# A state-space and attention stack in elements: first elements with their own banks, division of work and order

## The reference

```
xz = x @ in_proj; xb, z = split(xz)                    # 256 + 256 channels
xb = silu(causal_depthwise_conv(xb, 4 taps) + conv_b)  # called u in the kernel
proj = xb @ x_proj;  dt = softplus(proj[:8] @ dt_proj + dt_b);  b, c = proj[8:24], proj[24:40]
state = exp(dt * a) * state + dt * b * xb              # 256 channels x 16 states, along 512 tokens
y = (sum over states of state * c + D * xb) * silu(z);  return y @ out_proj
```

## Time and profile before

| | us |
|---|---|
| median of 3 runs | 2429.0 |
| lowest, highest | 2427.78, 2432.51 |
| profiled execution: its own time | 2435.31 |
| its span | 2433.5 |
| mean granted TensorE clock | 0.923 of full |
| busy: PE, DVE, ACT, POOL | 1903.3, 1883.9, 1767.4, 1715.1 |

### The profile page before, as it was taken

How to read it: one execution, slowest core, us unless ns; L and a number is a source line. 1 busy time by engine, 2 the same in 40 slices (tenths; PEclk the granted TensorE clock), 3 DMA queues, 4 the chain that set the end, 5 groups by cost and what they waited for, 6 DMA issues and landing times.

```text
span 2433.5 us, 43992 instructions
## 1 busy us (share of the span) xinstructions
PE 1903.3 (78%) x15823; PEld 1130.5 (46%) x15936; DVE 1883.9 (77%) x3461; ACT 1767.4 (73%) x3955; POOL 1715.1 (70%) x1572
## 2 busy tenths in 40 slices
PE   2246789796978879697878979698887979788866
PEld 0013455363635546363645536364544636364634
DVE  3557797979878797988879797987879798887442
ACT  2345778696978878696877869697887869686644
POOL 1969595977959596886959597795959688693110
PEclk7566999899999999998999989999999989999988
DMA  5444343535445343634535363544535263540100
GB/s 171 122 121 116 102 121 98 144 93 132 108 118 132 93 125 81 151 89 127 136 95 121 96 143 93 135 105 118 131 97 127 78 158 88 138 112 20 26 20 9
DMA packets 126345, 261.08 MB, mean 107 GB/s; under 512 B 26928, under 2 KB 59696, under 8 KB 125872
## 3 DMA queue, kind: packets, MB, share of 16 engines
q1 hardware_dynamic: 126128, 258.27, 40.9%
HBM read 185.42 MB, written 42.99 MB: 94 GB/s over the span
## 4 chain that ended last, share of the span: by engine, by line
PE 30%; POOL 24%; DVE 21%; ACT 13%; issue 8%; DMA 3%; SPq 1%; POOLq 0%; DVEq 0%; ACTq 0%
POOL dbu L662 9%; POOL gy L679 9%; DVE hs L634 4%; POOL kr L996 4%; PE b_bank L358 3%; PE f_bank L358 3%; DVE m L927 3%; ACT late L892 3%; DVE kr L941 2%; PE y_sum L585 2%; PE b_bank L719 2%; DMA spread<-steps 2%; DVE ss L914 2%; PE b_bank L745 2%; PE f_bank L1027 2%
## 5 line engine op out<-in xcount | busy, mean ns | idle before, releaser
L634 DVE TENSOR_TENSOR_SCAN hs<-da,dbu 128x512 f32<-128x512 f32 x512 | 623.2, 1217 | 101.4 <-POOL dbu L662 68.9
L662 POOL TENSOR_TENSOR dbu<-spread,bc 128x512 f32<-128x512 f32 x512 | 653.6, 1277 | 27.5 <-DMA spread<-steps 27.4
L679 POOL TENSOR_TENSOR gy<-hs,bc 128x512 f32<-128x512 f32 x512 | 652.7, 1275 | 22.4 <-DVE hs L634 10.6
L610 ACT ACTIVATE da<-spread,rest 128x512 f32<-128x512 f32 x512 | 364.3, 712 | 160.1 <-DVE hs L634 130.6
L996 POOL TENSOR_TENSOR kr<-kr,rn 128x512 f32<-128x512 f32 x256 | 264.5, 1045 | 23.3 <-ACT rn L850 13.2
L719 PE MATMUL b_bank<-rest,h_t 128*128 128x512 f32 x384 | 232.7, 716 | 60.3 <-DVE kr L941 56.3
L719 PE MATMUL f_bank<-rest,h_t 128*128 128x512 f32 x384 | 217.9, 666 | 25.9 <-DVE kr L941 17.9
L585 PE MATMUL y_sum<-gy,rest 128*32 128x512 f32 x1024 | 147.2, 650 | 101.0 <-POOL gy L679 101.0
L358 PE MATMUL b_bank<-first,kr 128*128 128x128 f32 x768 | 128.0, 292 | 109.1 <-DVE kr L941 90.5
L358 PE MATMUL f_bank<-first,kr 128*128 128x128 f32 x768 | 126.5, 291 | 72.8 <-DVE kr L941 65.4
L358 PEld LDWEIGHTS b_bank<-first,kr 128*128 128x128 f32 x768 | 89.3, 147 | 191.9 <-DVE kr L941 145.8
(11 more groups left out here) (172 smaller groups left out, 4884.6 us busy)
## 6 DMA issues: line engine op xcount, KB each, us to landing
spread<-steps SPq DMA_DIRECT2D x256, 512.0 KB, 5.2
vs<-v SPq DMA_DIRECT2D x96, 260.0 KB, 6.9
steps<-k_t SPq DMA_DIRECT2D x32, 512.0 KB, 3.3
bc<-bc_rows SPq DMA_DIRECT2D x32, 512.0 KB, 6.3
gate<-gates SPq DMA_DIRECT2D x32, 512.0 KB, 6.3
gates<-kr SPq DMA_DIRECT2D x16, 512.0 KB, 2.7
gates<-late SPq DMA_DIRECT2D x16, 512.0 KB, 3.4
vs<-v SPq DMA_DIRECT2D x32, 130.0 KB, 5.5
```

The source lines that it names most:

```text
L610: e.activation(da[:, :], spread[:, slot(b, s // 2), 0, :], ACT.Exp, scale=a_neg[:, s:s + 1]).then_inc(decayed.sem, 1)
L634: e.tensor_tensor_scan(hs[:, s % 2, :], da[:, :], dbu[:, s % 2, :], 0.0, ALU.mult, ALU.add).then_inc(scanned.sem, 1)
L662: e.tensor_tensor(dbu[:, s % 2, :], spread[:, slot(b, s // 2), 1, :], bc[:, s % 2, :], ALU.mult).then_inc(fed.sem, 1)
L679: e.tensor_tensor(gy[:, s % 8, :], hs[:, s % 2, :], bc[:, 2 + s % 2, :], ALU.mult).then_inc(read_out.sem, 1)
```

## The change

Five things change. Line numbers of the new code are given where they differ.

1. **Entry of element 0.** The four input products write four banks (`fa[0]`, `fa[1]`, `fa[2]`, `lb[0]`), the projection to b, c and dt a fifth (`lb[1]`), the two dt products `fa[0]` and `fa[1]` again. PE's waits on the convolution and on z fall away; the projection waits for u alone.
2. **Step inputs of element 0** (dt and du, four products) run on DVE at the end of its entry, not on GpSimd.
3. **Read-out by DVE.** In element 0 the scans with s % 3 > 0 (21 of 32), in element 1 those with s % 3 == 1 (11 of 32) have their product with c on DVE, one place behind the next scan. Scan s then waits on DVE's own read-out of s - 2, and two semaphores count the read-outs of elements 0 and 1.
4. **Decays.** In elements 0 and 1 odd scans take their decay from the bank `lb[0]`, even ones from `da`, so the decay s waits for scan s - 2 and no longer for s - 1. The back attention of element 0 waits for the last scan of element 1 before it uses `lb[0]`.
5. **Order in three parts.** Each engine has three words: the first covers the first five rounds, the second is repeated 11 times, the third holds the rest. The steps in each part add up to what the old word gave there, but for one or two steps at the seams; inside a round steps move.

```diff
+ROUNDS = 11
-def weave(word, late, **chains):
+def weave(first, usual, last, **chains):
+    for word in (first, *[usual] * ROUNDS, last):
...
+        def entry_bank(b, part):
+            if b:
+                return e_bank
+            return dict(turn=e_bank, i0=fa[0], i1=fa[1], i2=fa[2], i3=lb[0], x=lb[1], d0=fa[0], d1=fa[1])[part]
...
+                if b == 0 and h == NH2 - 1:
+                    for _ in step_inputs(E, e, 0):
+                        pass
...
-                E.wait_ge(*before)
-                e.matmul(e_bank[:, :], w_in[:, i * P:(i + 1) * P], xn_t, start=True, stop=True).then_inc(in_projected.sem, 1)
+                E.wait_ge(*(before if b else e_copied(0)))
+                e.matmul(entry_bank(b, f"i{i}")[:, :], w_in[:, i * P:(i + 1) * P], xn_t, start=True, stop=True).then_inc(in_projected.sem, 1)
                 yield
-            E.wait_ge(*z_made(b, 1))
+            E.wait_ge(*(z_made(b, 1) if b else u_made(0, 1)))
...
-                if h:
+                if h and b:
                     E.wait_ge(*dt_clipped(b, 0))
...
+        SHARED = 2
+        def by_dve(b, s):
+            return b < SHARED and (s % 3 > 0, s % 3 == 1,)[b]
...
+        def decay(b, s):
+            return lb[0] if b < 2 and s % 2 else da
...
-                if s:
+                if s and decay(b, s) is decay(b, s - 1):
                     E.wait_ge(*scanned(b, s - 1))
+                elif s > 1:
+                    E.wait_ge(*scanned(b, s - 2))
...
             for s in range(NSCAN):
+                if s > 1 and by_dve(b, s - 2):
+                    E.wait_ge(*reads(b, s - 2)[-1])
                 E.wait_ge(*decayed(b, s))
                 E.wait_ge(*fed(b, s))
...
+                if s and by_dve(b, s - 1):
+                    read_product(E, e, b, s - 1)
+                if s == NSCAN - 1 and by_dve(b, s):
+                    read_product(E, e, b, s)
                 yield
...
+                if bank is lb[0] and n == 2 and b == 0:
+                    E.wait_ge(*scanned(1, NSCAN - 1))
```

More of the change, by code:

```diff
@@ L94, in use_table @@
             self.e.preload_act_table_set(name)
-def weave(word, late, **chains):
-    late = {part[0]: int(part[1:]) for part in late.split()}
-    while chains:
+def weave(first, usual, last, **chains):
+    for word in (first, *[usual] * ROUNDS, last):
         for part in word.split():
             for _ in range(int(part[1:])):
-                if late[part[0]]:
-                    late[part[0]] -= 1
-                elif part[0] in chains and next(chains[part[0]], chains) is chains:
-                    del chains[part[0]]
+                next(chains[part[0]])
+    for chain in chains.values():
+        for _ in chain:
+            raise AssertionError("a step is left over")
 def build(nc, a, out):
@@ L412, in dve_enter @@
             for h in range(NH2):
+                bank = entry_bank(b, f"i{h}")
                 E.wait_ge(*pad_zeroed(b))
@@ L437, in pool_steps @@
                 yield
+        def pool_steps(E, e, b):
+            if b:
+                yield from step_inputs(E, e, b)
+            else:
+                for _ in range(2 * NH2):
+                    yield
         def pe_enter(E, e, b):
@@ L474, in act_enter @@
             for h in range(NH2):
+                bank = entry_bank(b, f"i{h}")
                 E.wait_ge(*in_projected(b, h))
-                if h:
+                if h and b:
                     E.wait_ge(*conv_step(b, 2))
-                e.activation(x_pad[:, h, NCONV - 1:], e_bank[:, :], ACT.Copy).then_inc(padded.sem, 1)
+                e.activation(x_pad[:, h, NCONV - 1:], bank[:, :], ACT.Copy).then_inc(padded.sem, 1)
                 E.wait_ge(*padded(b, h))
-                e.activation(e_bank[:, :], e_bank[:, :], ACT.Identity, bias=conv_b[:, h:h + 1],
+                e.activation(bank[:, :], bank[:, :], ACT.Identity, bias=conv_b[:, h:h + 1],
                              scale=conv_w[:, h, NCONV - 1:NCONV]).then_inc(tap_made.sem, 1)
@@ L497, in act_enter @@
                 E.wait_ge(*dt_projected(b, h))
-                e.activation(dt_abs[:, h, :], e_bank[:, :], ACT.Abs, bias=dt_b[:, h:h + 1]).then_inc(dt_size.sem, 1)
+                e.activation(dt_abs[:, h, :], entry_bank(b, f"d{h}")[:, :], ACT.Abs, bias=dt_b[:, h:h + 1]).then_inc(dt_size.sem, 1)
                 yield
@@ L509, in act_steps, with reads, read_product @@
             yield
+        SHARED = 2
+        def by_dve(b, s):
+            return b < SHARED and (s % 3 > 0, s % 3 == 1,)[b]
+        def reads(b, s):
+            if b >= SHARED:
+                return [read_out(b - SHARED, s)]
+            n = [0, 0]
+            for other in range(b + 1):
+                for step in range(s + 1 if other == b else NSCAN):
+                    n[by_dve(other, step)] += 1
+            return [sem(k - 1) for sem, k in ((pool_read, n[0]), (dve_read, n[1])) if k]
+        def read_product(E, e, b, s):
+            E.wait_ge(*c_loaded(b))
+            E.wait_ge(*scanned(b, s))
+            if s > 7:
+                E.wait_ge(*summed_up(b, 2 * (s // 8 - 1) + s % 2))
+            elif b > 0:
+                E.wait_ge(*x1_made(b - 1))
+            e.tensor_tensor(gy[:, s % 8, :], hs[:, s % 2, :], bc[:, 2 + s % 2, :], ALU.mult).then_inc(
+                (read_out if b >= SHARED else dve_read if by_dve(b, s) else pool_read).sem, 1)
         def group_rows(b, g):
@@ L543, in sp_state @@
             if b > 0:
-                E.wait_ge(*read_out(b - 1, NSCAN - 1))
+                for done in reads(b - 1, NSCAN - 1):
+                    E.wait_ge(*done)
             load_bc(1, c_loaded)
@@ L582, in pe_state @@
                     E.wait_ge(*skipped(b - 1, 1))
-                E.wait_ge(*read_out(b, 8 * (m // 2) + 6 + k))
+                for done in reads(b, 8 * (m // 2) + 6 + k):
+                    E.wait_ge(*done)
                 for j in range(4):
@@ L606, in act_state @@
                 E.wait_ge(*loaded(b, s // 2))
-                if s:
+                if s and decay(b, s) is decay(b, s - 1):
                     E.wait_ge(*scanned(b, s - 1))
+                elif s > 1:
+                    E.wait_ge(*scanned(b, s - 2))
                 E.use_table(EXP_LN)
-                e.activation(da[:, :], spread[:, slot(b, s // 2), 0, :], ACT.Exp,
+                e.activation(decay(b, s)[:, :], spread[:, slot(b, s // 2), 0, :], ACT.Exp,
                              scale=a_neg[:, s:s + 1]).then_inc(decayed.sem, 1)
@@ L672, in pool_state @@
                     yield
[L673 to L679 removed]
+                if not by_dve(b, s):
+                    read_product(E, e, b, s)
                 yield
```

31 lines of the change are left out of this document (10 added, 21 removed), and 81 rows, old and new, of the table ORDER.

## The result

| | before | after |
|---|---|---|
| median, us | 2430.8 (4 runs) | 2470.9 (4 runs) |
| lowest, highest | 2427.8, 2438.6 | 2464.1, 2474.5 |
| profiled execution, its span | 2435.3, 2433.5 | 2474.5, 2472.3 |
| ratio of after to before, 95% interval | | 1.0158 [1.0136, 1.0179] |

The change makes the kernel 1.6% slower. The forecast was 2389, so it missed by 82 us and named the wrong sign. The start gains 23.6 us up to element 3, as much as was forecast. The 11 usual rounds, which were to gain 1.3 us each, lose 5.4 us each.

A forecast was written before the change was run, and what follows sets the result against it. GpSimd was taken to set each scan stage's length, with latency chains between stages. Gains of 11 + 8 + 5 + 15.6 = 39.6 us off the median 2429.0 gave 2389.4 us, forecast range 2376 to 2400.

The forecast's parts named there:

- Entry: Element 0 up to its first read-out: more banks and step inputs on DVE gain 11 us, bounds 8 and 12.
- Scans of element 0: Scan stage of element 0: read-outs shared with DVE gain 8 us, ends a gain of 17 and a loss of 5.
- The chain given for undisturbed engines: Element 0's scans: tightest chain over three scans, 5.75 us, so 61.3 us for 32 scans, a gain of 16.5.
- Scans of element 1: Scan stage of element 1: 11 read-outs leaving GpSimd gain 5 us, ends 13 and minus 3.
- Start in all: Entry of element 0 and scans of elements 0 and 1 together: 24 us gained.
- only the start gains: Rival: entry and scans give 24 us, the usual round stays at 138.8; 2405 us in all, chance 24%.
- The usual round: Repeated rounds after the start: reordering removes waits, 1.3 us a round over 12 rounds, 15.6 us; ends 0 to 28.
- The prediction's own sign of being wrong: Forecast wrong if the usual round is 138.8 us or more, or element 0's `x1` comes later than 135.
- the 0.8: Usual round: `mr_x` runs ahead of GpSimd's L431, bringing both attentions and the first input product 0.8 us forward.
- The spread wait: Usual round: input products wait for spread loads issued behind the residual loads; moving those saves 1.5 us a round.
- The slower rival: Usual rounds: the clip moved up blocks DVE's queue; 3 us of stall a round gives 2441 us, chance 5%.
- The tail: Behind element 15: the chain is kept, no gain given, plus or minus 2 us.

The follow-up runs named there:

- old_rounds: The changed kernel with the old word of every engine in the 11 usual rounds, its first part kept; 2409.1 us, ratio 0.9905.
- win_late: The changed kernel with one pair of SyncE's window loads moved behind two spread loads and the input load in the usual rounds; 2423.6 us, ratio 0.9957.
- resid_new: old_rounds with the four residual loads alone at their new place, between the stores of dt and du; 2403.5 us, ratio 0.9891.
- new_rounds: The kernel before, with its own code and first five rounds, but the changed kernel's words from there on; 2505.8 us, ratio 1.0299.
- x_first: The changed kernel with only SyncE's input load moved, ahead of the two window steps in the usual rounds; 2461.9 us, ratio 1.0118.
- old_sp: The changed kernel with SyncE's old word in the usual rounds, new words on the four other engines; 2427.1 us, ratio 0.9982.
- win_early: The kernel before with a pair of SyncE's window loads, and two spread steps too, put ahead of the input load; 2510.3 us, ratio 1.0325.
- pe_act_new: old_rounds with the new usual words on PE and ACT alone; 2597.1 us, ratio 1.0694.

## Why the prediction was wrong

- **Entry: right in kind, a little too small.** Forecast 11 us with 12 as the upper bound, measured 58.36 - 45.44 = 12.9. The constant tables, which were to end at 44.3 and hold the first scan, ended at 42.6, and it started at 43.81. The split was off: the banks alone are 13.3 (10.0 forecast), the step inputs 0.8 at the first read-out (2.2 forecast). They don't add up, as the input products wait for the later of several things.
- **Scans of element 0: right.** Forecast 8 us with a stage of 70; measured 7.6 and 70.16. (The chain given for undisturbed engines starts with 2.65 us for 1.27 + 1.28 = 2.55, which changes its 16.5 to 17.5 and not the forecast.) The two rows of the read-out's line in the kernel after (ns min/median/max) show why it isn't 17:

```profile
L605 POOL TENSOR_TENSOR gy<-hs,bc x480: 1252/1272/1726, 45.4 to 2230.4; 128x512 f32<-128x512 f32 x160
L605 DVE TENSOR_TENSOR gy<-hs,bc x32: 666/668/1746, 49.2 to 227.1; 128x512 f32<-128x512 f32 x32
```

  The forecast said 0.7 alone and up to 1.9 beside GpSimd; it is 0.67 and up to 1.75. The reverse, which no row had shown, is there as well: GpSimd's products go from 1.27 to 1.73 us at most.
- **Scans of element 1: too small.** Forecast 5 us, measured 9.4 by the `x1` instants, within the bounds given (minus 3 to 13).
- **Start in all: right in size, in part by luck.** 24 us forecast, 23.6 at element 3. But the lead was 29.9 at element 1, 6 more than the sum, and 6.3 were lost again by element 3, which the forecast had no term for. Two misses of the same size cancel. The rival "only the start gains" (2405) is what old_rounds shows at 2409.
- **The usual round: the step that failed.** It reads "I take 1.3 a round over 12 rounds: 15.6 us". Measured is a loss of 5.4 a round over 11, 59 us: the term is 75 us off, and nearly all of the miss of 82. The prediction's own sign of being wrong, a usual round of 138.8 or more, came with 144.2. What the runs showed in its place is the transfer queue: window loads ahead of the spread loads and the input load cost 47 us (win_late), and the compute engines' new words 16 to 18 more. Of the two gains the causes went away as was said. `mr_x` no longer sits out L431:

```profile
L388 DVE SCALAR_TENSOR_TENSOR mr_x<-mv_x,rs_x x16: 152/153/276, 129.2 to 2245.8; 128x4 f32<-128x4 f32 x16
```

  But ACT had other work first and normalised `x1` 9.96 us after the sum (1108.59 - 1098.63), before 9.61, so the 0.8 never reached the first feed. The spread wait went, and other waits took the greater part of what it freed (resid_new). What decided was the sentence behind them, "Some 20 other steps per engine move as well, and each can put a wait where there was none". That was true, but it was given no price and no place, and the sum went on with the gains that had been looked for.
- **The slower rival: right in sign, wrong in mechanism.** It put a blocked queue on DVE's clip. The clip did wait, 0.7 us a round for ACT, far from the 2 us at which it was to decide, and its price of 2441 was 30 us short. The queue that blocked is SyncE's. Its order had been read for the residual loads alone; the window loads stand some ten rows ahead of them in the same order.
- **The tail:** 0 plus or minus 2 forecast, 3.1 lost, just outside.

Shown: the window loads' place is worth 47 us in the new kernel, more than its whole loss of 40 (win_late). That the usual words alone make the loss, without the new code, is shown by old_rounds and new_rounds. Within the 47 us the delayed spread loads and the slow landing of the input load were not priced apart: x_first was to do it and blocked the queue anew. Not settled: why the compute engines' new words cost a further 16 to 18 us (old_sp against old_rounds, 2427.1 - 2409.1; win_late against resid_new, (0.9957 - 0.9891) x 2431). Over ten rounds read-outs wait for scans 23.6 us (win_late) and not 8.0 (resid_new), and the last residual sum (`xs<-xs,v`) waits for ACT's norm 63.9 us and not 39.0. Which of the moved steps makes this, and whether the second wait costs anything, was not found. The worth of the second decay bank wasn't tried apart.

## What to carry to other kernels

When an order changes, read the queue that issues the transfers first, row by row: for each transfer that waits for an engine, list the loads that have come to stand behind it, and price the wait (here 14.7 us of silence) against when those loads are due. A wait that a profile puts down to a DMA has its cause in what stood ahead of that DMA on its queue; moving the one late load forward can show the next victim, or make one: a load that itself waits blocks all that stands behind it (x_first, win_early). Before a load is moved, look at what it waits for. And where words for several engines were made together, neither credit nor try one of them alone.

## What the hardware showed that was not expected

- GpSimd pays as well when DVE reads two SBUF operands, but less than a full wait. In the timeline of the kernel after, a DVE read-out starts at 51.01 and ends at 51.68; GpSimd's started 0.16 us behind it and took 1.63 us, 0.36 more than its 1.27, where 0.51 of the other were left:

```profile
51.01 0.67 DVE L605 TENSOR_TENSOR gy<-hs,bc 128x512 f32<-128x512 f32 x1
...
51.17 1.63 POOL L605 TENSOR_TENSOR gy<-hs,bc 128x512 f32<-128x512 f32 x1 [0.22 <-DVE hs L739]
```

  The Trainium skill ("SBUF — State Buffer", section "Who interferes with whom") calls the ports that VectorE and GpSimd share an exclusive lock, which whoever issues first gets for the whole instruction. The direction agrees; held for the whole read-out, GpSimd's would have taken 0.51 + 1.27 = 1.78 us and not 1.63.
- The landing time of one and the same load (256 KB) changes with what was issued just ahead of it: in the median 3.0 us before and 3.3 in win_late, but 8.2 after and 7.7 in new_rounds, where six other loads go out in the 4.2 us ahead of it.
- An order can cost 8% with the same instructions: pe_act_new and old_rounds differ in the sequence on PE and ACT alone, 1.0694 against 0.9905.
